# Two-layer attention kernel on one core: front end rebuilt, router and low-part work moved on GpSimd, flag load moved on TensorE

## What is computed

```python
# layer 0: x += local attention-free block of (layernorm(x) + ctx)
emb = x + pos_encod                      # here x = _layernorm(x), pos_encod = ctx
q = emb @ wq + bq;  k = emb @ wk + bk;  v = emb @ wv + bv
ek = jnp.exp(k - max_k);  ew = jnp.exp(w - max_w)   # w = pos_bias inside a band
y = jax.nn.sigmoid(q) * einsum(ew, ek * v) / einsum(ew, ek)
a = _layer_norm(y @ wo + bo + emb, gamma, beta)
out = _layer_norm(jax.nn.relu(a @ w1 + b1) @ w2 + b2 + a, gamma, beta)
# layer 0: x += quantised gated FFN of layernorm(x)  (w_gate, w_up, w_down)
# layer 1: x += masked attention of layernorm(x) over ctx, 16 heads of 8 columns
# layer 1: x += mixture of 8 experts of layernorm(x), one expert per token
wg_n = wg / jnp.maximum(jnp.linalg.norm(wg, axis=1, keepdims=True), 0.0001)
logits = (x @ w_red) @ wg_n.T            # router
h = gelu(x @ W1[e] + b1[e]);  o = (h @ W2[e] + b2[e]) * score
```

## Time and profile before

| | us |
|---|---|
| median of 3 runs | 263.34 (263.17 to 263.64) |
| the profiled execution's own time | 263.62 |
| its span (first to last instruction) | 261.8 |

### The profile page before, as it was taken

One profiled execution on the slowest core, in us unless ns is written; L12 is line 12 of the kernel. 1 busy time (PEld: TensorE's weight loads), 2 busy tenths in 40 slices (PEclk: granted clock), 3 DMA queues, 4 the chain that ended last, 5 costly groups with the idle time before them and its releaser, 6 DMA issues.

```text
span 261.8 us, 4575 instructions
## 1 busy us (share of the span) xinstructions
PE 198.6 (76%) x1646; PEld 129.2 (49%) x1646; DVE 195.1 (75%) x452; ACT 136.6 (52%) x272; POOL 119.6 (46%) x226
## 2 busy tenths in 40 slices
PE   0288596699833857728799998999996996999960
PEld 0067465489831236616344353444554883757420
DVE  6899796788567596944977768786935636679996
ACT  1256731394948657703477757876887256351000
POOL 2799553899664967770034876537004020000000
PEclk9999886779995559968979999999999999999995
DMA  5970040000400000000000000000000000000000
GB/s 162 405 314 4 0 156 5 3 0 4 160 3 0 1 0 0 3 5 3 0 0 0 4 1 4 0 3 0 0 4 3 0 3 0 4 0 20 23 20 20
DMA packets 3805, 8.72 MB, mean 33 GB/s; under 512 B 434, under 2 KB 2242, under 8 KB 3394
## 3 DMA queue, kind: packets, MB, share of 16 engines
q1 hardware_dynamic: 3312, 7.69, 8.0%
q10 hardware_dynamic: 468, 0.70, 0.8%
HBM read 7.86 MB, written 0.52 MB: 32 GB/s over the span
## 4 chain that ended last, share of the span: by engine, by line
PE 36%; DVE 34%; POOL 12%; ACT 7%; issue 6%; DMA 2%; SPq 1%; POOLq 0%; DVEq 0%
PE ps L1157 33%; DVE picksum L1122 5%; PE ps L1166 3%; POOL rstd L362 3%; DVE gate_pt L1116 3%; POOL w L374 3%; DVE rden L856 3%; DVE qd_mem L835 3%; DMA cst<-consts_dram 2%; DVE rows L784 2%; DVE mx L1010 2%; DVE gate_pt L953 2%; DVE amax L947 2%; ACT gate_pt L731 2%; DVE half_c L1000 1%
## 5 line engine op out<-in xcount | busy, mean ns | idle before, releaser
L1010 DVE TENSOR_REDUCE mx<-ps 128x2 f32<-128x512 f32 x64 | 42.3, 687 | 12.7 <-PE ps L1157 12.5
L731 ACT ACTIVATE gate_pt<-ps 128x512 f32<-128x512 f32 x64 | 37.1, 603 | 15.5 <-PE ps L1157 15.3
L504 POOL TENSOR_SCALAR gate_pt<-ka 32x256 f16<-32x256 f16 x64 | 25.5, 399 | 4.4
L1157 PE MATMUL ps<-gate_pt,half_c 128*128 128x512 f16 x64 | 25.0, 394 | 1.8 <-DVE mx L1010 0.9
L1157 PE MATMUL ps<-qb,gate_pt 128*128 128x256 f16 x128 | 25.3, 281 | 0.9
L491 POOL TENSOR_SCALAR spread<-mx 128x16 f16<-128x16 f32 x32 | 5.9, 202 | 36.5 <-DVE mx L1010 24.8
L1157 PE MATMUL ps<-gate_pt,hid_xm 128*32 128x256 f32 x256 | 20.4, 391 | 1.5 <-ACT gate_pt L731 1.5
L1157 PE MATMUL ps<-w,half_c 128*128 128x512 f16 x96 | 21.2, 380 | 0.0
L1157 PEld LDWEIGHTS ps<-qb,gate_pt 128*128 128x128 f16 x128 | 9.4, 99 | 18.8 <-issue 10.2
L1166 PE MATMUL ps<-cst,rows 128*128 128x128 f32 x32 | 7.6, 335 | 14.0 <-ACT rows L636 8.5
L362 POOL TENSOR_TENSOR rstd<-vareps,halfs 128x2 f32<-128x2 f32 x24 | 17.1, 713 | 2.0
(11 more groups left out here) (219 smaller groups left out, 544.7 us busy)
## 6 DMA issues: line engine op xcount, KB each, us to landing
stage<-weights_dram SPq DMA_DIRECT2D x2, 1024.0 KB, 7.3
wf<-weights_dram SPq DMA_DIRECT2D x4, 256.0 KB, 7.8
wf<-mask_dram SPq DMA_DIRECT2D x1, 1024.0 KB, 4.8
eb_oT<-ffw_dram SPq DMA_DIRECT2D x1, 768.0 KB, 7.8
ctx_in<-ctx_rows_dram ACTq DMA_DIRECT2D x1, 512.0 KB, 4.2
x_in<-x_dram SPq DMA_DIRECT2D x4, 128.0 KB, 4.9
gate_pt<-ctx_cols_dram SPq DMA_DIRECT2D x1, 512.0 KB, 8.1
out_dram<-ctx_in SPq DMA_DIRECT2D x4, 128.0 KB, 1.7
```

Source lines behind the costliest of these rows:

```text
L504: ins = nc.gpsimd.tensor_scalar(kz[part, n % KRING, k], ka[part, b, quad], 1.0, 0.0, ALU.mult, ALU.add)
L731: nc_act(pt[:, head % PRING].rearrange("p t n -> p (t n)"), ps[:, 2 + head % 2, :], ACT.Exp, scale=DK ** -0.5).then_inc(sig["probs"], 1)
L1010: V.tensor_reduce(mx[:, b, head:head + 2, t], score_bank(4 * n + i).rearrange("p (h n) -> p h n", h=2), AX.X, ALU.max).then_inc(sig["smax" ...
L1157: return nc.tensor.matmul(dst, lhsT, rhs, start=start, stop=stop, skip_group_check=True)
```

## The change

**Front end.** `gamma`, `beta`, `mbias` and the context leave the first places of ACT's queue: the context comes in four parts, the biases come as 64 rows of 128 in place of two rows of 2432, and the constants come in two parts (the identity and the small selector `esel` on ACT's queue, the rest on SP's). On SP's queue qkv comes right after x; `m1` and `m2` have a buffer each (`stage`, `stage2`), so m2's transfer waits for nothing. A bias is now added by one product with `brow16` (one row per 128 biases, high and low part) in which `esel`, a column with two ones repeated over the other side, picks the row; the q and k biases take two such products where one did. The large clears go from DVE to POOL. DVE splits the bias, interleaves statistics, centring and `emb` over the batches, and casts `id16`, `idbig` and the selector row after the low parts of `colsA`; POOL makes the low part of the qkv weights and no bias.

**Stage 3 and attention.** POOL's router steps go into n = 0, 1 and 2 of the attention, m1's low part goes there in quarters at n = 3 to 6, and m2's quarters move to n = 8, 9, 10 and 12.

**Flag.** DVE makes the flag after `kscale`, PE loads it after the second half of the keys, and the queries of batches 0 and 1 stand ahead of the branch.

```diff
+M1_AT = (3, 4, 5, 6)
+M2_AT = (8, 9, 10, 12)
...
-            sp.dma_start(cst[:, :], consts).then_inc(sig["l_cst"], 16)
+            sp.dma_start(wf32("qkv"), weights[:, SEG["qkv"][0]:SEG["qkv"][1]]).then_inc(sig["l_qkv"], 16)
+            sp.dma_start(cst[:, CSEG["iota"][0]:], consts[:, CSEG["iota"][0]:]).then_inc(sig["l_cst"], 16)
...
-            pool.wait_ge(sig["l_ctx"], 16)
-            for b in range(B):
-                pool.wait_ge(sig["rows_ready"], nth(R_IN, b))
-                nc.gpsimd.tensor_tensor(emb[:, b], rows[:, b], ctx_in[:, b], ALU.add).then_inc(sig["emb"], 1)
+            pool.wait_ge(sig["w_hi"], 1)
+            a, z = SEG["qkv"]
+            nc.gpsimd.tensor_tensor(w16[:, 1, a:z], wf32("qkv"), w16[:, 0, a:z], ALU.subtract).then_inc(sig["qkv_lo"], 1)
...
-            nc.gpsimd.tensor_scalar(bias16[0:2, cols], bias_h[:, cols], c("lo_2", 2), 0.0, ALU.mult, ALU.add)\
-                .then_inc(sig["bias_neg"], 1)
-            pool.wait_ge(sig["bias_neg"], 1)
-            nc.gpsimd.tensor_tensor(bias16[0:2, cols], bias16[0:2, cols], bias_in[:, cols], ALU.add).then_inc(sig["bias_rest"], 1)
...
-            split_lo("m1", 9)
...
+                if n < 3:
+                    router_part(2 * n)
+                    router_part(2 * n + 1)
+                if n in M1_AT:
+                    split_lo_quarter("m1", 9, M1_AT.index(n))
+                if n in M2_AT:
+                    split_lo_quarter("m2", 10, M2_AT.index(n))
...
-            act.dma_start(ctx_in[:, :, :, :], ctx_rows).then_inc(sig["l_ctx"], 16)
-            act.dma_start(gamma_b[:, :], gamma.partition_broadcast(P)).then_inc(sig["l_gb"], 16)
-            act.dma_start(beta_b[:, :], beta.partition_broadcast(P)).then_inc(sig["l_gb"], 16)
+            act.dma_start(ctx_in[:, 0], ctx_rows[:, 0]).then_inc(sig["l_c0"], 16)
             act.dma_start(bias_in[:, :], bias).then_inc(sig["l_bias"], 16)
-            act.dma_start(mbias_in[:, :], mbias).then_inc(sig["l_mbias"], 16)
+            act.dma_start(cst[:, 0:CSEG["iota"][0]], consts[:, 0:CSEG["iota"][0]]).then_inc(sig["l_id"], 16)
+            for b in range(1, B):
+                act.dma_start(ctx_in[:, b], ctx_rows[:, b]).then_inc(sig[f"l_c{b}"], 16)
...
-            def row_bias(dst, name, stop=True):
-                return mm(dst, ones16[:, 0:P], brow(name), False, stop)
+            def row_bias(dst, name, k=0, stop=True):
+                return mm(dst, chosen(name, k, P), brow16[:, :], False, stop)
+
+            def column_bias(dst, name, k):
+                return mm(dst, brow16[:, :], chosen(name, k, T), False, True)
...
+            pe.wait_ge(sig["flag_ready"], 3)
+            general = pe.value_load(flag_i[0:1, 0:1], min_val=0, max_val=B * T * T)
             for b in range(B):
                 pe.wait_ge(sig["rows_ready"], nth(R_ATT, b))
...
-            pe.wait_ge(sig["flag_ready"], 1)
+            for b in range(2):
+                queries(b)
             pe.wait_ge(sig["resmask"], 2)
-            general = pe.value_load(flag_i[0:1, 0:1], min_val=0, max_val=B * T * T)
```

237 lines of the change are left out of this document (135 added, 102 removed).

## The result

The changed kernel takes 255.70 us (median of 4 runs, 254.04 to 256.91) where the kernel before takes 263.49 (4 runs beside them, 263.17 to 264.14). The ratio is 0.9699, 95% interval 0.9648 to 0.9750. The forecast was 257.8. The profiled execution is the fastest of the four, 254.04 with a span of 252.2.

A forecast was written before the change was run, and what follows sets the result against it. No engine was full (PE 76%, DVE 75%), so stages where engines wait for each other bound the kernel. 263.62 - 1.3 - 3.1 - 4.0 + 2.85 = 258.1 profiled, 257.8 for the median; range 253.3 to 261.2.

The forecast's parts named there:

- Term 1: Front: earlier statistics and low parts of `colsA`, no bias work on POOL; 1.3 us gained, bounds 1 lost to 3.5 gained.
- the likelier case: Front: POOL's eight additions keep DVE's casts waiting until 19.1, band products start at about 30.2; 60 to 40.
- casts first: Front: DVE's cast gets in before POOL's additions, band products start at 27.9, 3.0 us gained.
- the early casts: Rival, front: casts get in before POOL's additions, front gains 3.0 in place of 1.3, time 256.1; 25 in 100.
- Term 2: Ahead of the outer norms: without router and m1 on POOL, x1 no longer waits for `rstd`; 3.1 us gained (2.3 to 3.4).
- Term 3: Flag: load hidden under the keys, first queries ahead of the branch; 4.0 us gained (2.0 to 6.0).
- the branch keeps its cost: Rival, flag: PE's sequencer reaches the branch only with the array, clock falls; flag gains 2.0, time 259.8; 18 in 100.
- Term 4: Attention: POOL's added router steps and quarters delay `spread` and two MoE norms; 2.85 us lost (1 to 4.5).
- the warnings: Signs of error: `esel` bias products well longer (0.1 each takes 3.2 back), first statistics after 7, DVE holding POOL in attention.
- POOL's work was exposed: Rival, attention: POOL's added 10.5 us isn't hidden, time 265.4 if all exposed, deciding from 8.4 on; 4 in 100.

The follow-up runs named there:

- the copy: The changed kernel run a second time, unchanged: 255.40 us, ratio 0.9722 to the kernel before.
- f2: Changed kernel with POOL's eight additions behind the row maxima and its position-band product behind all four `emb`: 255.06 us, ratio 0.9715 to the kernel before.
- f1: Changed kernel with POOL's eight additions waiting until DVE has taken the row maxima (`posmax`): 254.96 us, ratio 0.9711 to the kernel before.
- g2: Changed kernel with 22 products that nobody reads in PE's wait ahead of the band products: 254.81 us, ratio 0.9689 to the kernel before.
- e2: Changed kernel with the flag's register load put back directly ahead of the branch, behind the first two batches' queries: 257.86 us, ratio 0.9798 to the kernel before.
- e3: Changed kernel with the queries of batches 0 and 1 put back behind the branch, the load staying early: 260.78 us, ratio 0.9897 to the kernel before.
- e4: Changed kernel with the router's six steps and m1's whole low part put back ahead of the outer norms: 258.06 us, ratio 0.9800 to the kernel before.
- g4: Changed kernel with both the flag's load and the first two batches' queries put back: 260.92 us, ratio 0.9908 to the kernel before.
- f4: Changed kernel with the six router steps ahead of the first `spread` instead of at n = 0, 1 and 2: 254.19 us, ratio 0.9674 to the kernel before.
- f3: Changed kernel with m1's quarters at n = 3, 4, 5, 7 and m2's at 8, 9, 11, 13: 253.01 us, ratio 0.9642 to the kernel before.
- g1: Changed kernel with additions behind the row maxima, quarters at 3, 4, 5, 7 and 8, 9, 11, 13, router ahead of first `spread`: 253.79 us, ratio 0.9639.

## Why the prediction was right

The sum was 258.1 for a profiled execution; it is 254.04, and 254.90 in the copy. By terms:

**Term 1, 1.3 forecast: 0.94 at the band products, and 0.5 (copy) to 1.4 (first profile) behind them.** The casts were held, as the likelier case had it, and the band products start at 30.01 against 30.2. But two steps of the working were wrong. The statistics start at 6.29 and not 5.6, and the fourth `emb` was held for 1.6 more by two instructions of POOL that I had not looked at (f2 shortens it by 1.0 by moving one of them); the first product started at 15.53 and not 14.0, 0.24 later than before the change and not 1.3 earlier. And I priced the stretch behind it as if DVE's casts and `posmax` carried it. f1 takes the casts' hold away and gets 0.68, not the 2.3 that I had between "hold" and "casts first": PE is at its products from 15.5 to 27.4 with 0.45 idle. So the early casts, my first rival with 25 in 100, were worth nothing like 3.0. The two errors cancelled: the first product came 1.5 later than in the working and the stretch behind it was 1.7 shorter (14.48 for 16.2), so that 30.2 was met is in good part luck. The old kernel's diagonals did stand ahead of PE (0.86 and 0.19 of waiting); that loss is gone. What comes behind the band products is the clock: g2 shows 0.9 of it. The 0.5 that the copy too has over before is no sure gain: e2 and e3, with the same front and the same clock there, need 33.58 and 33.75, before 33.69.

**Term 2, 3.1 forecast: 3.35** (2.80 and 0.55), POOL idle ahead of `rstd`, nothing new late. e4 brings the wait back. Right in mechanism and size.

**Term 3, 4.0 forecast: 6.85** (0.56 and 6.29). This is the step that was mis-sized, over the far end of its bounds. The 2.85 between have two parts. First, at the scores 6.0 are gained against 4.0: 0.56 ahead of the low part, where DVE's own three small instructions for the flag lay and now end at 95.5 in idle time (the working had 0.6 for them), and 5.45 behind it (5.67 from low part to scores, before 11.12). I had put the branch's arrival in the middle between "ahead of the array" and "with it", and then taken 0.5 back for a low clock after a gap of 2 to 4. It was ahead: the 16 KB pass under the query products, these run at full clock (1.95 from the first to ACT's copy, before 3.59), and no low clock follows. What is left of the branch's cost is the 0.83 from the end of `half_c` to the scores (1.06 in the copy; 0.06 where the queries stand behind the branch, in e3, g4 and before). Second, 0.84 between scores and third shift product: the window from 129 to 133 before has a clock of 0.65, and after the change the clock is 1.00 all through that stretch. The working had put that at nothing. The rival "the branch keeps its cost" is refuted by the trace, and by e3 and g4, which bring the cost back by moving the queries alone or with the load.

The Trainium skill, "Runtime: NRT & Kernel Launch", section "Instruction fetch mechanics", has a taken branch whose target is not in the fetched window wait for its page. The trace agrees that a transfer of a page's size passes (82 GB/s in 0.2 us at 108.1) and that the first instruction behind the branch comes 2.6 after it. It also shows that the array need not stand still meanwhile: products queued ahead of the branch run on, and all but about 1 us of the wait lies under them.

**Term 4, 2.85 lost forecast: 2.89.** The router 0.83 (forecast 1.1; f4 gets 0.84 back), the two MoE norms 0.75 each (forecast 0.85 each; f3 gets both back). 0.55 came from a place that I had not named, the quarter at n = 12 beside the one-hot columns. The powers cost 1.65, as argued from the long one being a hold; e4 shows it long again (3.56) in the old place, ending at 55.86 beside the mask comparison's end at 55.80.

**What didn't come true of the warnings:** two bias products of 128 columns with the selecting operand take 0.27 to 0.28 together, as one old one of 256 did; DVE's statistics did not start after 7; POOL's work was exposed for 2.9 of 10.5 and not for 8.4.

So direction and mechanism were right in terms 2 to 4, and in term 1 for the hold but not for what carries the stretch. Against the first profile the sum is 4.1 too high: 2.85 from term 3, 1.0 from the front with its clock, 0.25 from term 2. The other three executions were slower than the profiled one, and the median missed by 2.1.

## What to carry to other kernels

Work that does not depend on a branch belongs ahead of it in the engine's own stream, enough of it to cover the branch's wait (here 3.6 us of products at full clock hid all but 0.8 to 1.1 of it): what matters is what is queued ahead of it, more than when the flag is loaded. Fewer products ahead, so that the engine meets the branch sooner, might give that last microsecond; no run tried it. When you move work into an engine's idle time, look at both neighbours: what starts right behind it in its own queue (the norm behind the quarter, 0.75) and which of VectorE's instructions with operands in SBUF run beside it (0.55 at the one-hot columns); a shift of three quarters by one place was worth 1.86 us. Before pricing a held instruction, ask whether another engine's chain carries the stretch; and a wait of TensorE can cost time behind it too, in clock: filling one of 2.6 us that could not be shortened gave 0.9.

## What the runs showed of the hardware

- A hold between GpSimd and VectorE can last through several instructions: `id16`'s cast 1.90, to the end of eight additions of 0.42. But it need not: in f1 a diagonal beside the same additions took 0.41, another 0.59, against 0.29 alone. In the kernel before the same kind took 1.79 beside them. The Trainium skill, "SBUF — State Buffer", section "Who interferes with whom", lets the two exclude each other for one instruction at a time, and says that a VectorE instruction with two SBUF inputs meets a reading one of GpSimd; the second part agrees with the `emb` of two SBUF tensors (2.21 in place of 0.61), the first with f1 and not with the changed kernel's cast. What decides which comes isn't settled here.
- The granted clock at the wait of 2.6 us of TensorE and behind it was 0.50 for 3 to 4 us in the copy, the kernel before, e2, e3, e4, f2 and g1, for about 7 us in f1, f3, f4 and g4, and 1.00 throughout in the first profile, with the same instructions as the copy; with the wait filled it was 1.00 in both runs. The front's products came to full rate at 17.9 to 19.2 whether they began at 14.62 (f2) or 15.65 (f1).
- A branch of TensorE costs 3.2 us of idle array when all the work stands behind it (e3), 4.0 with the register load right ahead of it too (g4), and 5.12 before the change with the load and the flag's own work ahead of it. The first instruction behind it starts 2.4 to 2.9 us after a 16 KB transfer has passed, in all 14 profiles. The register load itself takes 0.48 to 0.49, and 0.74 on the path.
- GpSimd's power takes 1.64 to 1.67 for 128x8 and mostly 0.69 to 0.71 for 128x2 (three of 24 take 0.77 to 0.88); for 128x8 it takes 3.52 and 3.56 beside VectorE's clip and mask comparison, and ends within 0.06 of the latter both times.
